# State-space mixer by channel tiles: gate, decay and half products laid out anew (one core)

## The reference, cut to what matters

```
x, B, C = silu(causal_conv4(in_proj(u)));  z = gate part of in_proj(u);  dt = softplus(...)
cum   = cumsum(dt * A)                      within a chunk
Ldec  = exp(cum_i - cum_j) for i >= j, else 0
y_intra = ((C_i . B_j) * Ldec * dt_j) @ x_j          per head
y_inter = (C * exp(cum)) @ state                     state carried from chunk to chunk
y     = y_intra + y_inter + D * x
out   = rmsnorm_per_group(y * silu(z)) * norm_w @ out_w
```

## Time and profile before

| | us |
|---|---|
| median of 3 runs | 2277.45 (2276.72 to 2279.14) |
| the profiled execution | 2285.04 |
| its span | 2283.3 |
| PE busy in it | 2109.0, 92% |
| DVE busy | 1667.0, 73% |
| ACT busy | 1443.2, 63% |
| POOL busy | 1130.3, 50% |

### The profile page before, as it was taken

How to read it: one execution, slowest core, us unless ns; L and a number is a source line. 1 busy time by engine, 2 the same in 40 slices (tenths; PEclk the granted TensorE clock), 3 DMA queues, 4 the chain that set the end, 5 groups by cost and what they waited for, 6 DMA issues and landing times. The chain is left out here.

```text
span 2283.3 us, 35195 instructions
## 1 busy us (share of the span) xinstructions
PE 2109.0 (92%) x10968; PEld 1645.1 (72%) x10968; DVE 1667.0 (73%) x2864; ACT 1443.2 (63%) x2823; POOL 1130.3 (50%) x976
## 2 busy tenths in 40 slices
PE   8999886899999999999999999999999999999868
PEld 4666575687777777777777777777777777777645
DVE  4777584677876787678768877877787778777766
ACT  1566524676667666766676677666766776677631
POOL 3545140455545564555465546564645465545531
PEclk9899997899999999999999999999999999999979
DMA  4000001312122212221222122212121222121110
GB/s 157 1 0 0 23 29 41 97 59 81 47 87 79 68 42 87 84 70 40 87 79 70 57 78 70 70 62 74 70 70 62 74 70 75 56 74 57 46 36 37
DMA packets 72231, 140.67 MB, mean 62 GB/s; under 512 B 34450, under 2 KB 35474, under 8 KB 67827
## 3 DMA queue, kind: packets, MB, share of 16 engines
q1 hardware_dynamic: 72050, 138.44, 18.4%
HBM read 134.74 MB, written 3.67 MB: 61 GB/s over the span
## 5 line engine op out<-in xcount | busy, mean ns | idle before, releaser
L92 PE MATMUL p_out<-w_out,yT 128*128 128x512 f32 x1536 | 391.5, 406 | 44.9 <-DVE yT L1452 38.7
L92 PEld LDWEIGHTS p_out<-w_out,yT 128*128 128x128 f32 x1536 | 298.1, 196 | 121.0 <-DVE yT L1452 43.4
L92 PE MATMUL p_mix<-x_high,w_x 128*128 128x512 f32 x1024 | 381.8, 434 | 1.4 <-DVE x_low L1028 1.4
L1607 POOL TENSOR_TENSOR wq_t<-wq_t,cb 128x1024 f32<-128x1024 f32 x128 | 325.2, 2541 | 108.5 <-DVE cb L1497 96.0
L764 DVE SCALAR_TENSOR_TENSOR conv<-p_mix,unit_small,conv 128x511 f32<-128x511 f32 (+2 forms) x384 | 287.3, 748 | 96.7 <-ACT conv L744 87.6
L92 PE MATMUL p_gate<-w_gate,x_high 128*128 128x512 f32 x1024 | 342.1, 416 | 13.7 <-POOL w_gate L1574 13.7
L1379 ACT ACTIVATE wq_t<-wq_t,minus_cum 128x128 f32<-128x128 f32 x1024 | 313.9, 389 | 1.4
L752 ACT ACTIVATE x_channels<-conv 128x512 f32<-128x512 f32 x128 | 80.6, 630 | 266.4 <-DVE conv L764 265.7
L1452 DVE TENSOR_TENSOR yT<-p_flip,yT 128x512 fp32r<-128x512 f32 x128 | 88.4, 691 | 216.0 <-ACT yT L1358 216.0
L1321 PEld LDWEIGHTS p_intra<-x_dt,wq_t 128*128 128x128 f32 x2048 | 241.1, 192 | 2.4
L1321 PE MATMUL p_intra<-x_dt,wq_t 128*128 128x64 f32 x2048 | 242.6, 272 | 0.0
(11 more groups left out here) (228 smaller groups left out, 4179.4 us busy)
## 6 DMA issues: line engine op xcount, KB each, us to landing
cum_all<-cum_rows SPq DMA_DIRECT2D x128, 512.0 KB, 3.7
w_staged<-in_w_gate SPq DMA_DIRECT2D x16, 1024.0 KB, 5.8
w_raw_tiles<-in_w_x SPq DMA_DIRECT2D x64, 256.0 KB, 3.7
w_staged<-in_w_out SPq DMA_DIRECT2D x16, 1024.0 KB, 4.8
w_raw_tiles<-in_w_bc SPq DMA_DIRECT2D x16, 256.0 KB, 2.9
x<-in_x SPq DMA_DIRECT2D x1, 2048.0 KB, 17.4
out<-z SPq DMA_DIRECT2D x8, 256.0 KB, 2.0
wqkv<-in_wqkv SPq DMA_DIRECT2D x4, 384.0 KB, 6.3
```

Source lines behind the costliest of these rows:

```text
L92: last = pe.matmul(dst, left[a](k), right[b](k), start=k == 0 and n_ == 0, stop=stop and k == tiles - 1 and n_ == 2)
L1607: pool.tensor_tensor(decay[:, k % 2], decay[:, k % 2], cb[:, c].unsqueeze(1).to_broadcast([P, UNIT_HEADS, P]), ALU.mult).then_inc(decay_do ...
```

## The change

The mixer's results stay with channels on the partitions. In detail:

- The gate is projected like x, by channel tiles of 128 and 512 tokens at a time, a half ahead, into `p_mix` and by silu into a buffer `SG` (attention's old one). One gate tile a step; the first four are made in `layer0_tail`.
- `flip_y` falls. y is [channels, tokens]; `p_y` sums carried and local part in PSUM: for each of 8 heads state[:, h] (128x64) as weights and the new `Ce` (C times exp(cum), 128 columns) moving, then x_dt[:, h] (128x64) as weights and the decayed scores (128 columns) moving. Heads alternate between PSUM partitions 0 to 63 and 64 to 127.
- `Ce` is a 512 KB broadcast DMA of exp(cum) in 12 of 16 steps (issued by SP once `inter_done` of the step before is there) and a product with C on POOL.
- Decay arguments: 8 Relu on ACT; then one Exp of 1024 columns. For odd steps they are made at the start of the step before (with the exponential), for even steps in the middle and at the end of the step before.
- The decayed scores are made on DVE, from the scores that PE turns once more into a bank `p_cb`; POOL's L1607 falls, as do DVE's L1442, L1512 and L1516.
- Squares: ACT squares y in place, DVE adds the four tiles (`tensor_reduce`), PE sums over partitions by one product of one column.
- All weight tiles (256 KB) go through four slots; high parts of x, gate and B/C by ACT, low parts by POOL. B/C's last tile moves from k = 0 to k = 2.
- The first half's products go through DRAM, 256 KB out and 256 KB back a chunk.

```diff
 # PE, one step
-    split_product(pe, p_gate[:], [x chunk parts], [w_gate parts], KT)
-    flip_y(*before)
-    pe.matmul(p_inter[:], BC[:, 1, cols], state[...])
+    channels("g")
+    channels("x")
+    wait(pe, decay_done, s)
+    pe.transpose(p_cb[:, 0:P], cb[:, c], ident[:]).then_inc(cb_flipped, 1)
+    pe.wait_ge(ce_done, n_carries(g, k) + 1)
+    wait(pe, y_sum, s)
+    for h in range(UNIT_HEADS):
+        m = pe.matmul(p_y[sides(h), h // 2], state[:, h], Ce[:, h], start=h < 2, stop=False)
+    channels("bc")
     project_out(*before); p_state
+    sum_squares(*before)
     flip_x
-        m = pe.matmul(p_intra[:, h * HEAD_P:(h + 1) * HEAD_P], decay[:, k % 2, h], xdt[:, h], ...)
+        m = pe.matmul(p_y[sides(h), h // 2], xdt[:, h], decay[:, k % 2, h], ...)
 # ACT, one step
+    split_high(*before)                      # copy of y to fp32r
+    if k % 2 == 0:
+        arguments(s + 1, k + 1)              # 8 x Relu
+        exponentials(s + 1, k + 1)           # 1 x Exp, 1024 columns
+    front.activate_gate(...)                 # silu into SG
+    squares(*before)
+    if 3 <= c < 3 + UT: high parts of one x tile and one gate tile
+    begin("x")
+    if k % 2 and more: arguments(s + 1, (k + 1) % STEPS)
+    end("x"); begin("bc"); end("bc"); keep_half; out_high_part at c == 0
+    empty_x(next)
+    if k % 2 and more: exponentials(s + 1, (k + 1) % STEPS)
 # DVE, one step
+    y_low_part(*before)
     Btok, cb (half 0)
+    add_squares(*before)
+    decayed_scores(s, k)                     # decay * p_cb, 1024 columns
     conv("x"); conv("bc")
     mean_square (half 1)                     # now waits for PE's sum_squares
     state update; y_sum; gate; out_sum (half 1); out_low_part at c == 0
 # POOL, one step
     xs; xdt
+    pool.wait_ge(in_exp_cum, (n_carries(g, k) + 1) * 16)
+    pool.tensor_tensor(Ce[:], Ce[:], C chunk over 8 heads, ALU.mult)
     xd (was x_skip)
-    decay * cb
     low parts; inverse_rms
```

More of the change, by code:

```diff
@@ L605, in __init__ @@
             self.steps.append(ev)
[L606 to L620, removed]
@@ L633, in emptied @@
[L633 to L638, removed]
-    def conv_parity(self, k, e):
[L641 to L653, removed]
+            g, p = g - 1, p + self.fills
@@ L1385, in group @@
-                        wait(act, y_done, s)
-                        act.activation(sg[:], p_gate[:], ACT.Silu).then_inc(sg_done, 1)
-                        before = (g if k else g - 1, (k - 1) % STEPS)
-                        if not (first and k == 0):
-                            empty_y(*before)
-                        if c == CHUNKS - 1 and not (last and half):
-                            gate_high_part(g * 2 + half + 1)
-                        target = 1 - half if c >= CPS else half
@@ L1400, in group @@
-                        for i, (e, fill, index) in convs:
-                            front.activate(act, e, index, PLAN.conv_parity(k, e))
-                        if not (first and k == 0) and before[1] < CHUNKS:
+                        started = not (first and k == 0)
+                        before = step_before(g, k)
+                        target = 1 - half if c >= CPS else half
+                        events = PLAN.events(k, last)
+                        more = k + 1 < STEPS or not last
@@ new lines, in group @@
+                        if k == CHUNKS - 1 and not last:
+                            for j in range(2):
+                                slot = BC_SLOT[j]
+                                front.high_by_act(act, front.bc_parts(j)[0], slot, raw_loads(g, 0, slot, 3), front.bc_w_high)
+                        begin("x")
+                        if k % 2 and more:
+                            if k + 1 == STEPS:
+                                act.wait_ge(logs_done, (g + 1) * 3 + 3)
+                            arguments(s + 1, (k + 1) % STEPS)
@@ L1484, in group, with conv @@
                         s = step(g, k)
+                        started = not (first and k == 0)
+                        before = step_before(g, k)
+                        cols = slice(c * P, (c + 1) * P)
                         mine = slice(half * UNIT_HEADS, (half + 1) * UNIT_HEADS)
-                        if k + 1 < STEPS:
-                            arguments(s + 1, k + 1)
+                        def conv(kind):
+                            for e in PLAN.events(k, last):
+                                if e[0] == kind:
+                                    front.run_taps(dve, e, PLAN.index(g, k, e), PLAN.bank(k, e), PLAN.conv_parity(k, e),
+                                                   1 - half if c >= CPS else half)
@@ L1882, in build @@
         with ExitStack() as lasting:
+            keep["wo_parts"] = [Named(nc, lasting).sb(f"w_o_{part}", [P, KT, DIM], F32R, side="right") for part in ("high", "low")]
             with ExitStack() as early:
```

685 lines of the change are left out of this document (397 added, 288 removed).

## The result

The changed kernel takes 2473.05 us in the median of 4 runs (2471.36 to 2475.88), the kernel before 2278.3 on the same chip: a ratio of 1.0845, 95% interval 1.0829 to 1.0861. It is 195 us slower, where 54 us faster was forecast, and outside the range. The profiled execution has a span of 2470.8 us against 2283.3. The mean granted clock of TensorE is 0.937 against 0.963. By the starts of the local products the difference of 187.5 lies as follows: 12.5 ahead of the first one (428.13 against 415.58), 174.8 between the first and the last of the mixer's 128 local products (1948.9 against 1774.1), 0.2 behind the last. So it is a matter of the step.

What follows compares the result with a forecast made beforehand. PE's work was taken as the bound, with the pair's chain giving back most of its gain: -48 us over eight groups and -6 at the ends, total -54, median 2277 to 2223 us; 8-in-10 range 2140 to 2340.

Steps and rivals of the forecast that it cites:

- the chain through a pair: Mixer, two steps' work followed across ACT, DVE, POOL and PE: a plain pair takes 23.8 to 25.2 us.
- PE's work: TensorE per mixer step: falls 0.89 us in a carrying step, 0.97 in the other four, 14.6 a group.
- Rival F: Local and carried products: two-strip products do not run side by side, +0.79 us each; 2325 to 2400 us, chance 0.07.
- Rival E: PE's changes of weight width cost 0.2 us each, 0.8 a step; 2274 to 2325 us, chance 0.07.
- Squares 0.63: ACT's squaring of y, last in its part of the pair's chain: 0.63 us, ending at D+6.5.
- D: Zero point of the pair's chain: the end of the gated y of step k-1, k even.
- Ce(k+1) at D+16.8, wanted at D+15.7, a microsecond: POOL's decay product of C for the odd step: ready at D+16.8 (17.3), so PE waits a microsecond for it.
- The sum of four tiles 0.6 (0.42 to 0.69): DVE's sum of the squares over four tiles, ahead of the decayed scores: 0.6 us, bounds 0.42 to 0.69.
- 31.0 instead of 30.96: Pair with a B/C tile on both steps, ACT adding 0.78+2.32+0.6: 31.0 us; with one tile 27.7 and 28.4.
- Ends: Before and after the mixer's steps: first gate weights' 4.95 us wait goes, last steps -1; -6 us (-15 to +10).
- Rival C: Running sums land late behind Ce's 512 KB broadcast, 1.6 us late in each of 64 pairs; 2325 us, chance 0.17.
- The group of 219: Eight pairs of mixer steps added up: 219.0 us against 225.4, 6.4 less a group.

Runs made afterwards that it cites:

- the doubled run: The kernel with four mends with its carried product issued twice in a row: 2378.94 us, ratio 1.0433.
- the kernel with all mends: Changed kernel with GpSimd's C product first, late turn of x, squares in their own tile, half 0 scores before y's low part, PE summing squares over tiles: 2356.7 us.
- the kernel with four mends: The kernel with all mends, but the sum of squares over the four tiles back on DVE as a reduction: 2361.83 us, ratio 1.0359.
- the early product: Changed kernel with GpSimd's decay product of C moved ahead of its two products on x_tokens: 2396.27 us, ratio 1.0505.
- the last one: The kernel with four mends plus B/C tiles on odd steps, half 1's squares summed on PE, half 0's scores ahead of the sum: 2276.45 us, ratio 0.998.

## Why the prediction was wrong, point by point

The step that failed is the chain through a pair: the order of the queues, and with it the waits. It gave 23.8 to 25.2 us for a plain pair, and the plain pairs measured 26.6 to 27.8. PE's work was mis-sized as well, which mattered less.

**PE's work** was forecast to fall by 0.89 us in a carrying step; it fell by 0.22 in half 0 (12.94 to 12.72, from k5 to k6 in both kernels) and by 0.26 in half 1 (12.65 to 12.39, from k9 to k10). The narrow part of that step of half 1 in the changed kernel:

```profile
1316.20 0.27 PE L1387 MATMUL p_cb<-ident,cb 128*128 128x128 f32 x1
1316.40 1.09 PE L1394 MATMUL p_y<-c_decayed,state 128*64 128x128 f32 x16
1317.43 3.04 PE L97 MATMUL p_out<-w_out,y_parts 128*128 128x512 f32 x12
1320.31 1.02 PE L1407 MATMUL p_state<-x_to_state,b_tokens 128*128 128x512 f32 x2
1321.17 0.28 PE L1355 MATMUL p_small<-one_column,square_sums 128*128 128x1 f32 x2
1321.31 0.63 PE L1336 MATMUL p_flip<-ident,x_channels 128*128 128x128 f32 x4
1321.87 1.09 PE L1422 MATMUL p_y<-wq_t,x_dt 128*64 128x128 f32 x16
1322.89 0.50 PE L97 MATMUL p_mix<-x_high,w_o_high 128*128 128x512 f32 x1
```

By starts: the turn of the scores 0.20 (forecast 0.11), each narrow product 1.03 and 1.02 (0.95 both), the output 2.88 (2.74), the squares 0.14 (0.10), the turn of x 0.56 (0.44). That is 0.09 + 0.15 + 0.14 + 0.04 + 0.12 = 0.54 above the working, and the gate and x tiles, put at no change, take 5.70 instead of 5.62. Together that leaves -0.27 of the 0.89, against -0.26 measured. Rival F is refuted (0.87 for sixteen more, the side-by-side end). Rival E had the right mechanism: 0.15 for a narrow product's two changes by the doubled run. The Trainium skill, "TensorEngine Tiling (Array Packing)", Key Properties, which says that changing the mode drains the engine, agrees with that. By these starts its price of 0.2 a change was not far off either, for what stands next to a narrow product is late as well: 0.09 for the turned scores, 0.14 for the output, 0.12 for the turn of x and 0.08 for the gate tile. These four were not tried by themselves. The prediction's reading that the earlier trace rows show no such cost rested on a modelled end of the products, which cannot show it. This step cost little, though. With the true work the forecast's pairs, which were already set by the chain, rise by 0.3 or less each.

**The chain** failed in five places.
- "Squares 0.63", 6.5 after D: the working let ACT square y without its wait for the low part. The kernel has that wait, because the squares are written in place. ACT stood 170.1 us before it. In its own tile: 26 us.
- The low part of y was not in the sum of the chain at all. Both its inputs are in SBUF now, and it takes 1.62 in the mean, since POOL's products stand beside it.
- "Ce(k+1) at D+16.8, wanted at D+15.7, a microsecond": in the steps with other work ahead of ACT's copy of x it was up to 4.6, 64.6 us of waiting in all; mended, 77 us, which may hold the shorter low part of y too. The prediction named this wait as the first one to look for, but as a harmless one, and took the order of POOL's queue as given.
- "The sum of four tiles 0.6 (0.42 to 0.69)" is 1.08, outside its own bounds, and it stands ahead of the decayed scores. Off DVE in half 1: 35 us; the scores ahead of it instead: 19.
- The turned scores `p_cb` stand in PE's queue ahead of the carried product, and PE waited 54.5 us for DVE to make `cb`, up to 6.9 at a time. The working gave this turn a price, 0.11, and no wait. In the kernel with all mends, where `cb` is ahead of the low part of y, the wait is 23.1; what that mend alone is worth in time was not run.

**What the prediction did not look at**: which bank a B/C tile gets. "31.0 instead of 30.96", "27.7 and 28.4" took such a step as a sum of ACT's work. In the kernel with four mends the even ones had PE wait up to 3.3 us for a bank that holds the gate's tile until ACT's silu behind arguments, exponentials and table: 47.6 us. Nor did it look at the turn of x in the fourth and eighth step of each half, which waits for a silu at the end of the same step: 13 us.

**Ends**: forecast -6, measured +12.5 at the front and 0.2 behind the last step. The front got the PE time of four gate tiles, some 11 us, and lost the wait of 4.95 for the first gate weights, as worked out. But PE's wait for its own sequencer at the mixer's entry went from 4.14 to 9.51 us, which the forecast did not have; why it did was not tried. At the back, the last steps, stripped of gate tiles, did not get shorter: in the kernel with four mends the last four take 12.3 to 13.9 us each, in the kernel before, with their gate products, 10.6 to 12.8. So the 11 us did not come back there.

**Rival C** had the right sign and the wrong place: the running sums landed later (4.3 us in the median, 6.4 at most, where 5.1 in every pair was the point at which it decides), but ACT waited for them only twice, 2.9 us in all, and 33.6 MB less changed nothing.

**What held**: the narrow products side by side, the decayed scores at 1211 ns (1.22), the Exp of 1024 columns at 1061 ns (1.0 to 1.06), the Relu group (312.1 us for 1024), table loads at 124. The group of 219 was near what a repaired order gives, 222.0, but that is in part luck: its first pair was forecast 6.0 us too short and its second 3.6 too long.

The mends sum as they were run: 2473 - 77 - 26 - 13 = 2357 (with four mends 2362), - 48 = 2314, - 35 - 3 = 2276. So 197 us went with places in the engines' queues, one tile and the engine of one sum. Two things are inside these terms and were not isolated: the lock between DVE and POOL (the low part of y is 1622 ns in the changed kernel, 981 with the early product, 1128 in the last one), and PE's clock, which is back at 0.963. The repaired kernel is still 53 us above the forecast of 2223.

## What to carry to other kernels

When work moves between engines, write each engine's new queue with every wait in it before pricing anything: most of the time lost here was an operation ready to run behind one that was not. Put first what needs the least (GpSimd's product of two early tiles), keep a reduction out of the queue ahead of what the next step waits for, and do not square or scale in place a tile that a slower engine still reads. And when an operand moves from PSUM to SBUF, look at what GpSimd does at that moment: here the pass alone stayed at 0.68 us and took 1.62 in the mean beside it.

## What the runs showed of the hardware that was not expected

- A DVE pass over two SBUF tiles that starts under a POOL product ended 0.54 to 0.55 us after that product in the three places read: 0.68 alone, 2.90 beside a product of 2.86. Means: 1622 ns, and 882 with that product cut to one head of eight. POOL's product of 1024 columns takes 2.35 to 2.94.
- A reduction over four tiles of 128 (512 elements in, 128 out, strided) takes 1078 ns on DVE, against 680 to 750 for other passes of 512 columns.
- Two-strip fp32 products of 128 columns cost 0.87 us for sixteen more, and going into and out of the form 0.15, beside the 0.08 to 0.14 by which the work next to them is late.
- The clock after a wait. PE stood 2.66 us before the turn of x at 1336.71. In the window behind it the granted clock is 0.63 (between its two levels, 0.5 for 1.2 GHz and 1.0 for 2.4), and 512-column products start some 0.43 apart until 1341.34, then 0.23 to 0.25:

```profile
1336.71:1341.34 4.63, 4.63 (x26) 3.58 (x27) 2.56 (x3) 3.58 (x5) 3.43 (x4) 0.63 0.83 242
```
```profile
1336.71 0.66 PE L1336 MATMUL p_flip<-ident,x_channels 128*128 128x128 f32 x4 [2.66 <-ACT x_channels L766]
```

The local product takes 1.32 from start to start in place of 1.02, and the six products behind it 2.72 in place of 1.51 in the step at 1322.89: this wait costs 1.5 us beyond its own 2.66.
